# Reordering the setup of a fused attention kernel, and splitting the first K projection of each batch in two

## What is computed

```python
x = L0_attn_hidden_states
xn = _layernorm(x, axis=-1)
qkv = hidden_states @ Wqkv_w.T + Wqkv_b            # hidden_states is xn
p = attn_map(q1, k1) - lam * attn_map(q2, k2)      # causal softmax of q k^T / sqrt(128)
o = einsum('bhqk,bkhe->bqhe', p, v);  o = o * rsqrt(mean(o*o) + eps) * subln_w * (1 - LAMBDA_INIT)
s = o.reshape(B, S, H * D) @ out_w.T + out_b
g = _silu(quant_dequant_mxfp4(xn) @ quant_dequant_mxfp4(weight).T + bias)
x = x + s * g
```

## Time and profile before

| | us |
|---|---|
| median of 3 runs | 1571.83 (1571.16 to 1575.48) |
| profiled execution, its own time | 1574.93 |
| its span in the trace | 1573.1 |
| PE busy in the span | 1480.6 |
| DVE, ACT, POOL busy | 1133.0, 889.5, 884.6 |

### The profile page before, as it was taken

How to read it: one execution, slowest core, us unless ns; L and a number is a source line. 1 busy time by engine, 2 the same in 40 slices (tenths; PEclk the granted TensorE clock), 3 DMA queues, 4 the chain that set the end, 5 groups by cost and what they waited for, 6 DMA issues and landing times.

```text
span 1573.1 us, 27528 instructions
## 1 busy us (share of the span) xinstructions
PE 1480.6 (94%) x8982; PEld 864.2 (55%) x8982; DVE 1133.0 (72%) x2654; ACT 889.5 (57%) x2474; POOL 884.6 (56%) x1588
## 2 busy tenths in 40 slices
PE   5877789999999999999999999999999999999998
PEld 2444345556555656455564655555655565645664
DVE  5888887767776777757777577766787578774772
ACT  4666775367633676347663577436773467634761
POOL 2565546565465555655556555656556565564554
PEclk9989899999999999999999999999999999999999
DMA  8246453334433453235532335344442345412442
GB/s 267 58 91 138 91 93 66 91 79 76 85 66 88 85 91 67 58 90 88 91 71 52 103 77 95 63 93 82 78 91 53 88 86 99 77 41 73 86 93 66
DMA packets 382448, 134.76 MB, mean 86 GB/s; under 512 B 361824, under 2 KB 365920, under 8 KB 382304
## 3 DMA queue, kind: packets, MB, share of 16 engines
q1 hardware_dynamic: 382304, 132.99, 40.5%
HBM read 35.93 MB, written 8.39 MB: 28 GB/s over the span
## 4 chain that ended last, share of the span: by engine, by line
PE 30%; DVE 27%; ACT 15%; POOL 14%; issue 8%; DMA 5%; SPq 1%; ACTq 0%; POOLq 0%; DVEq 0%
PE ps L555 9%; PE ps L556 8%; PE ps L557 8%; DVE ps L1032 6%; ACT pp L724 5%; DVE qkv L987 5%; DVE pp L1038 4%; ACT qkv L701 4%; DMA out_x<-res 2%; ACT on L746 2%; POOL qkv L1230 2%; ACT ph L733 2%; DVE aq L888 2%; POOL row L1278 2%; POOL row L1264 1%
## 5 line engine op out<-in xcount | busy, mean ns | idle before, releaser
L1264 POOL TENSOR_TENSOR row<-row,small 128x1 f32<-128x1 f32 x256 | 147.0, 574 | 414.7 <-ACT pp L724 414.7
L733 ACT ACTIVATE ph<-pp,small 128x128 f16<-128x128 f32 (+3 forms) x256 | 142.7, 557 | 315.9 <-DVE pp L1038 315.6
L555 PE MATMUL ps<-xT,wqkv 128*128 128x512 f16 x768 | 296.3, 386 | 26.1 <-DMA xT<-gate 10.2
L724 ACT ACTIVATE pp<-ps,row 128x384 f32<-128x384 f32 (+3 forms) x512 | 268.2, 524 | 61.9 <-DVE row L1032 56.9
L556 PE MATMUL ps<-xT,wqkv 128*128 128x512 f16 x768 | 296.4, 386 | 0.0
L557 PE MATMUL ps<-xT,wqkv 128*128 128x512 f16 x768 | 295.6, 385 | 0.0
L1032 DVE CUSTOM_DVE_ANT_0 ps<-ps,mask,ssc 128x384 f32<-128x384 f32 (+3 forms) x512 | 261.9, 552 | 9.5 <-PE ps L624 8.5
L987 DVE SCALAR_TENSOR_TENSOR qkv<-ps,bsc,qkv 128x512 f16<-128x512 f32 x192 | 143.5, 750 | 115.9 <-ACT qkv L701 115.8
L1050 DVE SCALAR_TENSOR_TENSOR on<-ps,row,on 128x256 f16<-128x256 f32 x256 | 123.7, 483 | 122.8 <-ACT on L746 119.5
L555 PE MATMUL ps<-qkv,pT 128*128 128x256 f16 x640 | 176.1, 275 | 29.4 <-DMA pT<-ph 21.2
L1044 DVE SCALAR_TENSOR_TENSOR ph<-pp,small,ph 128x128 f16<-128x128 f32 (+3 forms) x256 | 157.7, 616 | 61.7 <-ACT ph L733 60.9
(11 more groups left out here) (140 smaller groups left out, 2983.2 us busy)
## 6 DMA issues: line engine op xcount, KB each, us to landing
wqkv<-in_wqkv SPq DMA_DIRECT2D x15, 512.0 KB, 6.8
xin<-in_x SPq DMA_DIRECT2D x7, 1024.0 KB, 5.9
xres<-in_x SPq DMA_DIRECT2D x28, 256.0 KB, 3.4
out_x<-res SPq DMA_DIRECT2D x28, 256.0 KB, 2.4
vbias<-in_bv SPq DMA_DIRECT2D x32, 128.0 KB, 3.2
pT<-ph SPq DMA_TRANSPOSE x256, 2.8
wout<-in_ow SPq DMA_DIRECT2D x8, 512.0 KB, 4.3
heads<-on SPq DMA_TRANSPOSE x128, 3.2
```

Source lines behind the costliest of these rows:

```text
L555: mm(out, ah, bh, start=start and j == 0, stop=False)
L724: run(out, sc_ps[u][:, m, 0:w], ACT.Exp, bias=ebias[:, u, m:m + 1], scale=-1.0, accum_out=psum_l[:, n % 6, m:m + 1]).then_inc(exp_done, 1)
L733: run(ph[:, n % PH, 0:w], pp[:, 1 + u, 0:w], ACT.Copy, scale=sigma).then_inc(ph_hi, 1)
L1264: pt(recip, l2, minusone, ALU.pow).then_inc(recip_done, 1)
```

## The change

PE makes `norms` of tiles 1 to 3 ahead of the first fill instead of behind it, and `norms` of tiles 4 to 7 behind the scores of step 0 instead of behind those of step 1. ACT squares tiles 4 to 7 one after each of the first four fills, where two of them came after the sixth and seventh entry. DVE makes the scales of group 1 directly behind the maxima of step 0, ahead of the sixth fill, and `w_low(4)` ahead of both V fills. The first K projection of each batch is made in two halves of 256 tokens, each behind its own `xT_done`.

```diff
-SETUP = [("norm", 0), ("warm", 10), ("fill", 0), ("norm", 1), ("fill", 1), ("fill", 2), ("fill", 3), ("fill", 4),
-         ("scores", 0), ("fill", 5), ("fill", 6), ("scores", 1), ("norm", 2), ("fill", 7)]
+SETUP = [("norm", 0), ("warm", 10), ("norm", 1), ("fill", 0), ("fill", 1), ("fill", 2), ("fill", 3), ("fill", 4),
+         ("scores", 0), ("norm", 2), ("fill", 5), ("fill", 6), ("scores", 1), ("fill", 7)]
...
-                    last = split3(bank, [((wqkv[:, t, 0, a, ch], wqkv[:, t, 1, a, ch]), (xT[:, :, 0, a, :], xT[:, :, 1, a, :]))
-                                         for a in range(NC)])
+                    wide = NT // 2 if (kind, g, j) == ("k", 0, 0) else NT
+                    for k in range(0, NT, wide):
+                        if wide < NT:
+                            pe.wait_ge(xT_done[k // wide], 16 * (f.b + 2))
+                        last = split3(bank[:, k * P:(k + wide) * P],
+                                      [((wqkv[:, t, 0, a, ch], wqkv[:, t, 1, a, ch]),
+                                        (xT[:, k:k + wide, 0, a, :], xT[:, k:k + wide, 1, a, :])) for a in range(NC)])
...
             fill(FIRST[0])
+            square(4)
             w_high(2)
             fill(FIRST[1])
+            square(5)
             w_high(3)
             fill(FIRST[2])
-            square(4)
+            square(6)
             fill(FIRST[3])
-            square(5)
+            square(7)
             fill(FIRST[4])
             exps(0, 1)
             exps(0, 0)
-            square(6)
             fill(FIRST[5])
-            square(7)
+            w_high(4)
             for a in range(1, AHEAD):
+                p_hi(a - 1)
                 exps(a, 1)
-                p_hi(a - 1)
                 exps(a, 0)
             fill(FIRST[6])
-            w_high(4)
             fill(FIRST[7])
...
             quantise_early(1)
+            squares(2)
             fill(FIRST[4])
             maxima(0, 1)
             maxima(0, 0)
-            fill(FIRST[5])
-            squares(2)
-            quantise_early(1)
-            for a in range(1, AHEAD):
-                maxima(a, 1)
-                combine(a - 1)
-                maxima(a, 0)
-                p_lo(a - 1)
-            fill(FIRST[6])
             dve.wait_ge(su_norm, 3)
             take(junk[0], 4)
             scales(2)
             score_scales(1)
+            fill(FIRST[5])
+            quantise_early(1)
+            for a in range(1, AHEAD):
+                combine(a - 1)
+                maxima(a, 1)
+                maxima(a, 0)
+                p_lo(a - 1)
             w_low(4)
+            fill(FIRST[6])
             fill(FIRST[7])
```

More of the change, by code:

```diff
@@ L649, in _ @@
                 elif kind == "fill":
-                    if n == 0:
-                        for j in range(2):
-                            pe.wait_ge(xT_done[j], 16)
                     fill(FIRST[n])
@@ L661, in _ @@
                 for f in PLAN[n]:
-                    if f.kind == "k" and f.g == 0 and f.j == 0:
-                        for j in range(2):
-                            pe.wait_ge(xT_done[j], 16 * (b + 2))
                     fill(f)
```

## The result

| | us |
|---|---|
| changed kernel, median of 6 runs | 1562.71 (1560.43 to 1564.78) |
| kernel before, median of 6 runs beside it | 1571.91 (1570.72 to 1575.75) |
| ratio | 0.9933, 95% interval 0.9919 to 0.9946 |
| span of the profiled execution | 1560.4 (before: 1573.1) |

The change makes the kernel 0.7% faster, 9.2 us by the medians. The prediction said 1560.0, from 1554.5 to 1567.0.

The account below looks back on a forecast made before the run. DVE's V chain, not PE, was taken to set the pace of setup and batch 0. Setup 8.2 us plus later boundaries 3.5 gave 11.7 off; from the median of 1571.83 that is 1560.1, stated as 1560.0, range 1554.5 to 1567.

Parts of the forecast that it names:

- The order of the bounds: End of setup: PE reaches group 1's K 10.3 us earlier, but DVE's second V step, 8.2 us earlier, sets the gain.
- Part 1: Setup, sum ahead of first fill: DVE copies at 20.2, 6.7 us earlier; `w_high(1)` begins at 21.5.
- Part 2: Setup halves: first half begins at 19.6 instead of 21.68; DVE finishes the first fill at 26.1, 5.8 us earlier.
- Parts 3 and 4: Setup: squares between evictions put `w_high(2)` 4.9 us earlier; group 1's earlier scales bring PE to its K near 44.6.
- The rival with late loads: Setup: tile 4 landing at 28.6 holds ACT, `w_high(2)` 3.3 us later than forecast, total 1563.5; 5%.
- Passing through batch 0: Batch 0: the setup's 8.2 us gain passes through, bounds 6 and 10.3.
- The rival that half is given back: Batch 0 swallows half of the 8.2 us and the boundaries give nothing: 1568; 10%.
- Part 5: Halves at seven later boundaries: gains 1.3, 1.3, 1.1 at second to fourth, 0 elsewhere, less 0.2 cost: 3.5 us.
- rivals with a larger gain (1552.5): Full clock in the first fill, less half clock in batch 0, and all boundaries passing: 7.5 us more; 12%.
- halves that don't overlap (1592): Later first K projections: each half costs 0.27 us instead of 0.11, 28 us over seven batches; 4%.

Follow-up runs that it names:

- group 1 alone: Kernel before with only group 1's squares, sum and scales and tile 4's low part moved; no halves, first sum stays behind the first fill: 1572.06 us, 0.9979.
- second and third profile: The unaltered changed kernel run again in two later sets beside the kernel before: 1564.42 us (0.9933) and 1561.19 us (0.9923).
- rounding step later: Changed kernel with DVE's early rounding step behind the scales of tiles 1 to 3 instead of ahead, run twice: 1563.09 us (0.9918) and 1559.97 us (0.9912).
- order only: Changed kernel without any halves, the first K projections waiting for both transposes again: 1567.10 us, 0.9956.
- halves in the setup only: Changed kernel with the seven later batches' first K projections whole again, with the old waits: 1567.80 us, 0.9954.
- halves alone: Kernel before, its order kept, with only each batch's first K projection made in halves, the setup's too: 1569.78 us, 0.9969.
- quantiser step in the gap: Changed kernel with DVE's last three setup quantiser steps placed between its two V steps: 1566.49 us, 0.9939.
- second place for V: Changed kernel with fill 7's V product written to the unused fourth tile of `gate`, so DVE's second V step needn't wait for POOL: 1562.66 us, 0.9929.

## Why the prediction was right

**The order of the bounds.** Right. PE was ready for group 1 at 44.70 (forecast 44.6), 10.2 us earlier, and DVE's V chain was the bound that counted: 46.44 against a forecast of 46.5, 8.2 us. The run with group 1 alone shows the difference between the two bounds: PE's 4 us wait removed, 2.1 us of the V step gained. That the two times meet to 0.06 us is in part luck: this trace's first scale copy is 0.38 us later than in the trace of before, and part 1 had a miss that cost little here.

**Part 1, half wrong.** The copy came at 20.48 (forecast 20.2). But `w_high(1)` began at 23.85, not 21.5, and its low part ended at 26.81, not at about 24.5. I took the 1.34 us between copy and `w_high(1)` from the earlier trace rows, where POOL was idle; moved to 20.5, the same steps stand beside POOL's rounding, which the trace of before has in about the same place as the new one. I had moved an instruction past another engine's queue without asking what runs there. The price could be read in the trace of before, too: the last scale step of group 1 (L850, 128x4, at 51.14) took 1.00 us there instead of 0.17, beside POOL's row. In the profile of after the miss is nearly hidden, by luck with the clock: the first fill ran at the 1.2 GHz level until 23.4 and ended near 24.4, so ACT, which took it at 25.03, could have had it only some 0.5 us sooner. `w_high(2)` began at 26.91, 0.5 us later than forecast, 0.4 of which is that trace's later first copy. In the second and third profile the first fill's halves stood 0.11 us apart from the start, it ended near 23.6 and 23.2, and yet `w_high(2)` began 12.3 us behind the first copy in all three: there the stretched scale steps held it, not PE. By the runs with the rounding step later the miss costs 0.4 us at the V step when the first fill runs at the lower level and 1.2 us when it runs at the upper one.

**Part 2.** First half at 20.05 (19.6), DVE's part of the first fill ended at 27.48 (26.1). On top of the order, the halves in the setup moved V by 3.1 us in the traces (34.95 to 31.8 in the last column of the table); the medians of order only and halves in the setup only, 1567.10 and 1567.80, don't show it. Scatter of the later batches is as large.

**Parts 3 and 4.** `w_high(3)` at 29.58 (29.3), fill 4's end near 35.35 (35.1) and the sum at 35.69 (35.5), the copy at 37.48 (37.3), `w_high(4)` at 39.25 (39.0), `w_low(4)` ended at 43.80 (43.7). All within 0.3 us. The rival with late loads didn't occur.

**Passing through batch 0.** Right, by the table: 8.2 us at V, 8.1 at the first boundary (215.35 to 207.25); counted from the first copy 8.6 at V, and 8.5, 8.6 and 8.1 at the boundary in the three profiles. The rival that half is given back is out.

**Part 5, the boundaries.** The size was near, but the pattern isn't borne out. PE's wait at the first boundary for both causes together went from 3.59 us to 3.42, so swallowed as said. From the rows at the others the waits shrink from 1.99 to 1.02 at the second (1.0 us, forecast 1.3) and from 2.00 to 0.30 at the fourth (1.7, forecast 1.1). I had said 0.7 us would remain in the middle of the projection; nothing did. The gate waits at the last three are 0.45, 1.20 and 1.17 where xT and gate together made 0.78, 0.83 and 0.78. But a shorter wait is a gain only if nothing behind it takes the time back, and the lengths of the stretches in all fourteen profiles tell more. From the first boundary to the end, the five kernels without later halves take 1358.0 us on the mean (1356.3 to 1359.0), the nine profiles with them 1355.5 (1352.0 to 1357.9): 2.5 us for the halves, forecast 3.5. Only 1.0 of it lies before the fourth boundary (562.2 and 561.3 on the mean, ranges that overlap), where 3.7 were forecast, and 1.6 behind it (795.8 and 794.2), where 0 was. Between the second and third boundary nothing was gained (186.5 and 187.3): PE's waits for pT grew from 1.9 to 4.2 us there. I had asked what comes next behind each first K projection only as far as the gate step. By whole runs the later halves are worth 3.4 us (changed against halves in the setup only), forecast 3.5; from halves alone, 5.4 less the 3.6 that its first boundary came earlier, it is 1.8. The 2.5 from the profiles lies between these.

**The total.** 11.7 us were forecast from the profiled execution, and its successor's span is 12.7 shorter; the medians give 9.2, 10.7 and 12.5 us in the three comparisons. The forecast lies in this spread. Of the 2.7 us between 1560.0 and 1562.71 about 1 is the later halves' term, and the rest is no more than the scatter of executions: profiles of the same changed kernel have spans of 1560.4, 1565.3 and 1563.5. Between the first and third boundary they take 374.2, 379.1 and 378.0 us. In the second of these two batches PE's waits for pT were 2.8, 5.1 and 4.6 us, which is most of the difference there; what makes them vary stays open. The rivals with a larger gain (1552.5) and with halves that don't overlap (1592) are out: the halves stand 0.11 us apart at 763 us. (That last rival's sum has a slip: 24 times 0.27 us is 6.5 and not 6.6 us, which makes it 1590.5.)

## What to carry to other kernels

Two engines can both be late at the end of a stage; count what the second one lets through, not what the first one gains, and test it by a marker behind both (here a step at 207 us) rather than by the total, whose scatter was as large as the parts. Count such markers from an early event of the same trace: that brought 1.0 us of scatter at the second V step down to 0.02. When steps are moved earlier, read the other engines' timelines at the new place: a step of 0.17 us cost 1.27 there. A transfer that was waited for in halves is best used in halves, but what it gives is to be measured over the whole batch: here a part came back as other waits.

## What the runs showed of the hardware

Many DVE steps that work on SBUF alone last longer when a 128x512 POOL instruction on SBUF runs beside them, up to almost the whole of its length: 128x3 in 1.27 and 1.11 us instead of 0.17 beside POOL's 1.26 and 1.27, a combine in 1.25 instead of 0.35, a 128x512 integer step in 1.60 instead of 0.69, and the low part below in 2.35 instead of 1.28. It goes the other way too: with the rounding step later, POOL's L1207 took 2.24 us from 22.99, beside DVE's 128x1024 step from 22.82. Not every step is hit: the layer norm's statistics of the next batches (L963, one 128x512 input in SBUF) start seven times inside such a POOL instruction in the changed kernel and take 0.66 to 0.69 us, as they do alone. In the changed kernel, DVE and then POOL:

```profile
50.57 2.35 DVE L928 SCALAR_TENSOR_TENSOR wqkv<-wqkv,heads 128x1024 f16<-128x1024 f32 x1
```

```profile
50.58 1.26 POOL L1209 TENSOR_TENSOR xin<-xin,res 128x512 f32<-128x512 f32 x1
```

The long step grew by 1.07 us, most of POOL's 1.26. The Trainium skill (SBUF — State Buffer, SBUF: two separate sides) says that DVE and GpSimd (POOL) share one pair of ports, held for a whole instruction by whoever starts first, the other fully blocked; on DVE's side it names instructions with two SBUF inputs, against a GpSimd instruction that reads SBUF, and those in a 2-port perf mode. The traces agree for steps that start behind POOL (L844 at 20.67 ends with POOL's instruction at 21.9) and for the statistics, which have one input; in which mode L844 ran, no trace shows. The 2.35 us step started 0.01 us ahead of POOL's and was the one that grew; by their recorded starts this isn't the order of that rule, and no run here tells whether the records or the rule are finer than that.

The same contention undid two edits that looked free in a timeline (the quantiser step in the gap and most of the second place for V). A gap on one engine was worth little because another engine's instruction filled it.

In the first profile of the changed kernel the granted clock is recorded as 1.00 for the stretch from 19.6 to 24.7 us although the matmuls stood at the spacing of the 1.2 GHz level up to 23.4. There the spacing, not that record, tells the level.
